# A fused transformer on one core: a second batch's shared expert moves from the second program into the first, and the addresses of the expert table with it

## The chip, the cores and the metric

The kernel runs on one core of a Trainium2 chip. The metric is the time of one launch in device microseconds. Before the change the median of 3 runs is 1389.91 us (1389.63 to 1391.88).

## What is computed

Four batches of 512 rows with 256 features go through an encoder-decoder layer (masked self-attention, cross-attention, a feed-forward net of 1024), an int8 linear layer, a second cross-attention, and a mixture of experts. All attentions have 16 heads of 16 features. The last stage is the one that the change touches. Per row `xf` (already normalised):

```
logits = xf @ router.T                 # 16 experts, the best 2 are taken, weights by softmax
gu     = xf @ gate_up[e]               # 256 -> 512, for the two experts of the row
h      = silu(gate) * up
moe    = sum over the two experts of weight * (h @ down[e])
sg, su = x @ shared_gate.T, x @ shared_up.T          # 256 -> 512 each, for every row
shared = (silu(sg) * su) @ shared_down.T             # 512 -> 256
out    = residual + moe + shared
```

All products are in f32, except attention's scores, which are stacks of bf16 parts.

## The kernel before

The kernel has two programs (two blocks of engine instructions), one behind the other.

**The first program** holds everything up to the router. Its order is written out by hand: `batch_order()` puts named operations on steps, four places to a step, and every engine walks through the same list `ORDER` and emits what is its own. A step is one key tile of one group of four heads: TensorE makes four score tiles (`score_t`, two PSUM banks in turn), ScalarE takes their exponentials, TensorE multiplies the step before with V (`values`, at place 2 of a step). Other products (projections, transposes, the router) are laid between these by `place(step, ...)` and share two PSUM banks, `bankM`: a product waits until the bank's last reader has read. `END[n]` is the last step of attention `n` (12 of them, three for each batch); attention 11 is batch 3's last. Behind it comes a tail for batch 3: transposes, the output projection, a residual add (`add` on VectorE), row statistics, normalisation (`apply` on ScalarE), a transpose (`turn`), the router's `logits`, `top`, `rank`, `route` on VectorE, and `dispatch` on GpSimd, which scatters (token, weight) pairs into the table `tag_scr` in HBM. Among these stands the shared expert of batch 0: products `gate` and `up` for each of 4 slices `m` of 128 hidden features, `swish` (SiLU on ScalarE), `hid` (VectorE multiplies), then `down` and `sadd`, which adds the product to the residual rows `acc`. `EARLY_SHARED` says how many batches are treated so.

**The second program** (`experts`) has the shared expert of the other `LATE = B - EARLY_SHARED = 3` batches on TensorE: per batch 4 slices of gate and up, with the last batch's `down_products` behind the first slice of the next. Meanwhile VectorE works out from the counts `cnt` which rows of the table belong to each of 47 tiles of 128 tokens (`places`), GpSimd reads these rows by an indirect DMA (`table`), TensorE turns them (`turn_table`, after slice `TURNED_AT`), and VectorE makes token addresses of them (`addresses`). SyncE starts the 32 transfers of all experts' weights (12.6 MB) when the table has landed, then writes `acc` to `out`. GpSimd gathers the rows of each tile (`rows(s)`, 128 rows of 1 KB), every second one of them held back by a wait on the shared expert's progress. `homes` says which buffer a tile's rows go to, `homes_free` from which slice on it is free: the buffers behind the first 33 are those of the shared expert's operands.

**The expert tiles.** When all of `hid`, the weights (`w_in`) and the first rows are there, TensorE goes through 47 tiles: gate and up product, the turn of the rows two tiles on, and the down product of the tile before. ScalarE copies the weights of the tile's expert into `w_now` two tiles ahead (`stage`), makes SiLU and scales the result by the row's weight into `yt`. GpSimd adds `yt` to `out` by an indirect DMA with accumulation, one for each tile, in order; it may start when `acc` has landed in `out` (`rows_out`). A tile of another expert than the one before may name the same rows, so SyncE lets GpSimd on (`apart`) only when the transfer of the tile before has landed; tiles of one expert follow without this wait.

## Time and profile before

| what | value |
|---|---|
| median of 3 runs | 1389.91 us |
| the profiled execution's own time | 1395.61 us |
| its span, first to last instruction | 1393.5 us |
| mean granted TensorE clock | 0.966 |
| PE busy | 1262.2 us (91%) |
| DVE busy | 872.2 us (63%) |
| ACT busy | 709.7 us (51%) |
| POOL busy | 521.4 us (37%) |
| first program ends, second begins | 1166.87 us |
| first product of an expert tile | 1242.82 us |
| first addition of an expert tile to `out` | 1253.59 us |

The busy shares are means over stages with different limits, and busy PE time contains stretches at half the clock. So the last 310 us are read by stretches below: the last steps of attention (from 1084.53), the tail of the first program (from 1120.56), the shared expert of the second program (from 1166.87) and the expert tiles (from 1242.82).

### The profile page before, as it was taken

How to read it: one execution, taken by the hardware profiler on the slowest of the kernel's cores; microseconds unless marked ns; L12 is line 12 of the kernel's file. 1: busy time of each engine (PE TensorE's matmuls, PEld its weight loads, DVE VectorE, ACT ScalarE, POOL GpSimd, SP SyncE). 2: the span in 40 equal slices, each digit the busy share in tenths (PEclk: the TensorE clock that was granted, in tenths of full speed). 3: DMA queues.
4: the chain of work that ended last, by engine and by line, in shares of the span. 5: the costliest groups of instructions: out<-in, count | busy, mean ns of one | idle time of the engine just before them, and what ended most of it. 6: DMA issues, size and time to landing. Idle time of an engine off the chain costs nothing. (4 is left out here: it accounts for less than half of the span.)

```text
span 1393.5 us, 19214 instructions
## 1 busy us (share of the span) xinstructions
PE 1262.2 (91%) x6164; PEld 616.7 (44%) x6164; DVE 872.2 (63%) x1998; ACT 709.7 (51%) x1290; POOL 521.4 (37%) x731
## 2 busy tenths in 40 slices
PE   6899989989999999999999999998899879889996
PEld 4232432323343224453443453443332344559995
DVE  5889779788877886458566567568777423112221
ACT  2345455566545654556556456455656631026663
POOL 4444251153312411326226236235323214655545
PEclk8699999999999999999999999999999989999998
DMA  8473413424331333123123123115431002963331
GB/s 254 135 241 83 148 58 81 117 69 142 111 106 24 107 92 106 35 73 106 47 62 107 46 61 107 51 57 127 132 98 33 17 15 83 367 151 40 37 36 13
DMA packets 113219, 131.58 MB, mean 94 GB/s; under 512 B 17017, under 2 KB 93305, under 8 KB 112867
## 3 DMA queue, kind: packets, MB, share of 16 engines
q1 hardware_dynamic: 102867, 119.91, 29.4%
q0 software_dynamic: 10256, 10.45, 4.8%
q8 instruction: 52, 0.85, 0.3%
q14 instruction: 44, 0.36, 0.1%
HBM read 83.25 MB, written 48.40 MB: 94 GB/s over the span
## 5 line engine op out<-in xcount | busy, mean ns | idle before, releaser
L1287 DVE TENSOR_REDUCE Mx<-bank 128x1 f32<-128x512 f32 x512 | 338.7, 684 | 206.6 <-PE bank L1021 202.8
L903 ACT ACTIVATE prob<-bank 128x512 f32<-128x512 f32 x576 | 332.2, 594 | 260.7 <-PE bank L1047 255.7
L1047 PE MATMUL bank<-QS,KS 99*128 99x512 bf16 x768 | 296.0, 387 | 39.0 <-ACT prob L903 20.6
L1021 PE MATMUL bank<-KS,QS 96*128 96x512 bf16 x768 | 298.3, 390 | 12.9 <-DVE Mx L1284 6.3
L1060 PE MATMUL bank<-prob,V 128*17 128x512 f32 x1536 | 206.6, 610 | 1.7 <-issue 1.7
L903 ACT ACTIVATE prob<-prob 128x512 f32<-128x512 f32 x192 | 120.9, 630 | 158.8 <-DVE prob L1298 157.9
L1047 PEld LDWEIGHTS bank<-QS,KS 99*128 99x128 bf16 x768 | 74.7, 98 | 233.8 <-ACT prob L903 127.1
L1021 PEld LDWEIGHTS bank<-KS,QS 96*128 96x128 bf16 x768 | 76.1, 99 | 123.7 <-issue 48.5
L1284 DVE CUSTOM_DVE_ANT_0 bank<-bank,ff_h 128x512 f32<-128x512 f32 x128 | 87.9, 696 | 21.7 <-PE bank L1021 21.1
L740 POOL TENSOR_SCALAR parts<-rest 128x512 bf16<-128x512 f32 x47 | 29.1, 620 | 184.1 <-DVE rest L1247 183.5
L1594 POOL DMA_INDIRECT out<-yt,home x47 | 73.1, 1555 | 64.7 <-SPq L1551 40.0
L726 POOL TENSOR_SCALAR shift<-mv 128x4 f32<-128x4 f32 x28 | 5.5, 196 | 239.9 <-DVE mv L1208 239.9
L1284 DVE CUSTOM_DVE_ANT_0 bank<-bank,mask 128x512 f32<-128x512 f32 x128 | 87.1, 701 | 10.7 <-PE bank L1021 10.2
L1685 PE MATMUL ebank<-xT,hid 128*128 128x128 f32 x752 | 92.2, 275 | 1.4 <-issue 0.9
L1685 PEld LDWEIGHTS ebank<-xT,hid 128*128 128x128 f32 x752 | 91.2, 192 | 4.7 <-issue 2.3
L749 POOL TENSOR_SCALAR MR<-neg 16x128 bf16<-16x128 f32 x48 | 14.3, 297 | 205.0 <-ACT neg L878 204.9
L973 PE MATMUL bank<-hT,mask 128*128 128x512 f32 x160 | 78.9, 622 | 4.6 <-DVE T L1389 3.5
L1799 DVE TENSOR_TENSOR ht<-ebank,sgt 128x256 f32<-128x256 f32 x47 | 20.0, 425 | 98.5 <-ACT sgt L1621 93.6
L1298 DVE TENSOR_TENSOR prob<-bank,ff_h 128x512 f32<-128x512 f32 x96 | 65.7, 684 | 12.6 <-PE bank L1047 12.2
L984 PE MATMUL bank<-mask,ff_h 128*128 128x256 f32 x288 | 68.1, 381 | 5.2 <-DVE rest L1247 4.4
L973 PE MATMUL bank<-hT,w_qkv 128*128 128x512 f32 x128 | 68.7, 625 | 4.1 <-DVE rest L1247 3.8
L1298 DVE TENSOR_TENSOR prob<-bank,mask 128x512 f32<-128x512 f32 x96 | 65.6, 684 | 10.0 <-PE bank L1047 9.8
(183 smaller groups left out, 1866.9 us busy)
## 6 DMA issues: line engine op xcount, KB each, us to landing
stack_scr<-parts SPq DMA_DIRECT2D x48, 384.0 KB, 2.6
QS<-stack_scr SPq DMA_DIRECT2D x47, 384.0 KB, 4.3
KS<-stack_scr SPq DMA_DIRECT2D x47, 384.0 KB, 5.2
stack_scr<-parts SPq DMA_DIRECT2D x48, 256.0 KB, 2.9
w_gu<-in_gate_up SPq DMA_DIRECT2D x16, 512.0 KB
stack_scr<-parts SPq DMA_DIRECT2D x48, 128.0 KB, 2.9
cT<-in_ctxT SPq DMA_DIRECT2D x8, 512.0 KB, 5.8
w_dn<-in_down SPq DMA_DIRECT2D x16, 256.0 KB
```

The costliest lines, as they stand in the source:

```text
L740: link(pool.tensor_scalar(s[:, 1, :], r, 1.0, 0.0, ALU.mult, ALU.add))
L903: act.activation(prob[:, u % NP_, j, :], src, ACT.Exp, scale=CAST).then_inc(exp_done, 1)
L973: ins = pe.matmul(b[:, :], w[:, kd, m * P:(m + 1) * P], src[:, kd, :], start=(kd == 0), stop=(kd == KD - 1))
L984: ins = pe.matmul(b[:, i * D:(i + 1) * D], src[:, k, t * P:(t + 1) * P], w[:, k, :], start=(k == 0), stop=(k == nk - 1))
L1021: pe.matmul(m, QS[0:STACK, h, qt * P:(qt + 1) * P], KS[0:STACK, h, :], start=True, stop=True).then_inc(s_full, 1)
L1047: pe.matmul(bankT[e % NT][:, :], KS[0:ROWS, h, kt * P:(kt + 1) * P], QS[0:ROWS, h, :], start=not on_pe, stop=True).then_inc(t_full, 1)
L1060: ins = pe.matmul(bankO[32 * j:32 * j + VW, :], V[VALUES[n]][:, kt, g * HG + j, :], prob[:, u % NP_, j, :], start=(kt == 0), stop=(kt == Q ...
L1284: dve.tensor_tensor_reduce(b, b, mb[n % 2][:, qt, :], 1.0, -3.0e38, ALU.add, ALU.max, dst).then_inc(s_read, 1)
L1287: dve.tensor_reduce(dst, b, AX.X, ALU.max).then_inc(s_read, 1)
L1298: dve.tensor_tensor(prob[:, u % NP_, j, :], bankT[e % NT][:, :], mb[n % 2][:, QT + u % QT, :], ALU.add).then_inc(t_masked, 1)
L1594: pool.indirect_dma_start(sums, bass.IndirectOffsetOnAxis(home[:, s:s + 1], 0), yt[:, s % NY, :], None, bounds_check=SLOTS - 1, oob_is_err ...
L1685: ins = pe.matmul(bank[2 + s % 2][:, m * P:(m + 1) * P], w_now[:, s % 2, k, m * P:(m + 1) * P], xT[:, s % 3, k, :], start=(k == 0), stop=( ...
```

## The change

`EARLY_SHARED` goes from 1 to 2: batch 1's shared expert leaves the second program. In the first, batch 1 takes the places in the tail that batch 0 had, and batch 0's eight products (`gate` and `up` of 4 slices) go among the last eight steps of attention 11. VectorE copies each out of its PSUM bank (`keep`: gates into `held_gate`, which lies in weights no longer used, ups into `hid[0]`). Behind attention ScalarE takes SiLU of all four gates in one instruction (`silu`), VectorE multiplies all four slices (`mul`), and batch 0's two `down` halves stand before and behind `rank`. `places()` moves behind the last `route` in the first program, with its tiles, and the fill of `table` to the first program's start; the table's read is the first instruction of GpSimd in the second program, and it is turned after the first slice and not the third. GpSimd gathers 32 tiles' rows ahead and not 47; the other 15 follow one behind each of the first 15 additions.

The diff, cut (the removed lines of `places` and of the tiles' declarations in `experts` are those that stand in the first program now):

```diff
-EARLY_SHARED = 1
+EARLY_SHARED = 2
...
             if n == NB - 1:
-                for m, step in enumerate((1.5, 2.5, 3.75, 5.5)):
-                    place(e + step, ("gate", 0, m), ("up", 0, m))
...
+                jobs = [(what, 0, m) for m in range(HT) for what in ("gate", "up")]
+                for i, job in enumerate(jobs):
+                    place(END[n] - 7 + i, job)
+                    place(END[n] - 6.75 + i, ("keep", *job))
+                place(e + 0.5, ("silu", 0))
+                place(e + 0.75, ("mul", 0))
+                for m, step in enumerate((1.5, 2.5, 3.75, 6)):
+                    place(e + step, ("gate", 1, m), ("up", 1, m))
+                for m, step in enumerate((1.75, 2.75, 4, 6.25)):
+                    place(e + step, ("swish", 1, m))
+                for m, step in enumerate((2.25, 3.25, 4.5, 6.5)):
+                    place(e + step, ("hid", 1, m))
+                for q, half, step, gap in ((0, 0, 4.75, 0.75), (0, 1, 5.5, 0.25), (1, 0, 6.75, 0.25), (1, 1, 7.25, 0.25)):
+                    place(e + step, ("down", q, half, 0), ("down", q, half, 1))
+                    place(e + step + gap, ("sadd", q, half))
...
+    if kind == "keep":
+        return "dve", [tuple(at)]
...
+        held_gate = w_qkv[:, 0:2, :, :, :].rearrange("p a w k n -> p (a w k n)")[:, 0:HT * S]
...
+                    elif kind == "silu":
+                        read_done(act, ("gate", at[0], HT - 1))
+                        act.activation(held_gate, held_gate, ACT.Silu).then_inc(gates_done, 1)
...
-                        read_done(pe, ("up", p, HT - 1))
+                        if p == 0:
+                            pe.wait_ge(hid_ready, 1)
+                        else:
+                            read_done(pe, ("up", p, HT - 1))
...
+                def places():
...
+                    dve.tensor_tensor(table_row[:, :], which[:, :], before_it[:, :], ALU.subtract).then_inc(row_ready, 1)
...
+                def keep(what, p, m):
+
+                    dst = held_gate[:, m * S:(m + 1) * S] if what == "gate" else hid[p][:, m, :]
+                    left(dve.tensor_copy(dst, bank_of((what, p, m))[:, :]), (what, p, m))
+
+                def multiply(p):
+
+                    dve.wait_ge(gates_done, 1)
+                    read_done(dve, ("up", p, HT - 1))
+                    h = hid[p].rearrange("p m n -> p (m n)")
+                    dve.tensor_tensor(h, h, held_gate, ALU.mult).then_inc(hid_ready, 1)
...
+                        if p == B - 1:
+                            places()
...
-        TURNED_AT = (0, 2)
+        TURNED_AT = (0, 0)
+        FREE, AHEAD = 10, 32
...
-        homes_free = NX * [0] + 4 * [HT] + 4 * [2 * HT] + 8 * [3 * HT]
+        homes_free = NX * [0] + 4 * [HT] + 4 * [2 * HT] + 8 * [LATE * HT]
...
-                pool.wait_ge(consts, 4)
                 pool.wait_ge(row_ready, 1)
                 pool.wait_ge(tagged, 32 * TT)
                 pool.indirect_dma_start(table[:, :, :].rearrange("s p c -> s (p c)"), None, table_of,
                                         bass.IndirectOffsetOnAxis(table_row[0:TILES, 0:1], 0),
                                         bounds_check=NE * SLOTS // P - 1, oob_is_err=False).then_inc(table_in, 16)
...
-                for s in range(TILES):
-                    if s >= ROWS_SEM and s % 2 == 0:
-                        c, i = divmod((s - ROWS_SEM) // 2, QT + HT)
+                for s in range(AHEAD):
+                    if s >= FREE and (s - FREE) % 2 == 0:
+                        c, i = divmod((s - FREE) // 2, QT + HT)
                         if i < QT:
...
+                    if AHEAD + s < TILES:
+                        rows(AHEAD + s)
...
-                places()
                 for c in range(LATE):
                     for m in range(HT):
                         n = c * HT + m
                         dve.wait_ge(sg_done, n + 1)
                         dve.tensor_tensor(hid[:, c % 2, m, :], bank[(n % 2) * 2 + 1][:, :], sg[:, n % 2, :],
                                           ALU.mult).then_inc(hid_done, 1)
-                        if n == 0:
+                        if (c, m) == TURNED_AT:
+                            addresses()
                             tile_experts()
                         if c and m == 0:
                             add_shared(c - 1)
-                        if (c, m) == TURNED_AT:
-                            addresses()
```

TensorE's queue at the tail of the first program, from the last slice before the router to the end of the program. `hT,mask` are the shared expert's gate and up products, `mask,ff_h` its down products, `w_router` the logits, `both` the ranks. Before:

```order
L973 MATMUL bank<-hT,mask 128x512 x4
L1160 MATMUL bank<-w_router,hT 128x16 x8
L1169 MATMUL bank<-both,before 128x16
...
L1169 MATMUL bank<-both,ones_b 128x16 x4
L973 MATMUL bank<-hT,mask 128x512 x4
L984 MATMUL bank<-mask,ff_h 128x256 x16
L536 UNCONDITIONAL_BRANCH
```

and now:

```order
L1000 MATMUL bank<-hT,mask 128x512 x4
L1192 MATMUL bank<-w_router,hT 128x16 x8
L1011 MATMUL bank<-mask,ff_h 128x256 x8
L1201 MATMUL bank<-both,before 128x16
...
L1201 MATMUL bank<-both,ones_b 128x16 x4
L1011 MATMUL bank<-mask,ff_h 128x256 x8
L1000 MATMUL bank<-hT,mask 128x512 x4
L1011 MATMUL bank<-mask,ff_h 128x256 x16
L558 UNCONDITIONAL_BRANCH
```

Sixteen more down products stand there, half of them between the logits and the ranks. Each f32 product of these lists is two instructions in the trace.

TensorE's queue in the last steps of attention (`QS,KS` score tiles, `prob,V` the product with V, `identf,oT` the turn of attention's output). Before:

```order
L1047 MATMUL bank<-QS,KS 128x512 x4
L1060 MATMUL bank<-prob,V 17x512 x4
L1047 MATMUL bank<-QS,KS 128x512
L1060 MATMUL bank<-prob,V 17x512 x4
L1084 MATMUL bank<-identf,oT 128x128 x4
```

and now:

```order
L1074 MATMUL bank<-QS,KS 128x512 x2
L1000 MATMUL bank<-hT,mask 128x512 x2
L1074 MATMUL bank<-QS,KS 128x512 x2
L1087 MATMUL bank<-prob,V 17x512 x4
L1074 MATMUL bank<-QS,KS 128x512
L1087 MATMUL bank<-prob,V 17x512 x4
L1111 MATMUL bank<-identf,oT 128x128 x4
```

One gate or up product of batch 0 (two rows of the list) stands among the score tiles of a step; seven more stand so in the seven steps before.

GpSimd's queue in the second program, from its start into the additions. Before:

```order
L1562 IOTA landed 1x48
L1567 DMA table<-tag_scr,table_row 47x256
L1578 DMA xr<-t_scr,token 128x256 x33
L1578 DMA hT<-t_scr,token 128x256 x8
L1578 DMA mask<-t_scr,token 128x256 x6
L1594 DMA out<-yt,home 2048x256 x47
```

and now:

```order
L1620 IOTA landed 1x48
L1630 DMA xr<-t_scr,token 128x256 x32
L1646 DMA out<-yt,home 2048x256
L1630 DMA xr<-t_scr,token 128x256
L1646 DMA out<-yt,home 2048x256
L1630 DMA hT<-t_scr,token 128x256
```

Fifteen gathers stand between additions now, and the table's read stands ahead of this piece, before the two IOTAs.

## Rows read from the trace of the kernel before

**Rows 1.** Busy time by stretch: from:to and length, engines' busy us, PEclk, DMA share, GB/s.

```profile
1084.53:1117.49 32.96, 26.30 (x149) 8.90 (x148) 12.18 (x51) 21.38 (x43) 9.00 (x14) 0.90 0.06 18
1120.56:1133.27 12.71, 10.40 (x37) 7.53 (x38) 1.37 (x3) 3.07 (x4) 0.00 (x0) 0.60 0.00 0
1150.81:1158.33 7.52, 6.67 (x23) 2.74 (x23) 2.18 (x8) 1.88 (x2) 3.98 (x4) 0.63 0.01 2
1166.87:1242.82 75.95, 67.92 (x199) 39.35 (x199) 18.70 (x47) 9.17 (x14) 43.44 (x49) 0.93 0.78 259
1253.59:1297.64 44.05, 44.05 (x342) 42.51 (x341) 11.46 (x31) 28.06 (x47) 23.39 (x16) 1.00 0.38 43
```

**Rows 2.** Timeline of POOL, expert tiles: start, us, line, operation [idle before, releaser].

```profile
1253.59 1.64 POOL L1594 DMA_INDIRECT out<-yt,home  x1 [4.24 <-DMA out<-acc]
...
1265.58 1.55 POOL L1594 DMA_INDIRECT out<-yt,home  x1 [2.85 <-SPq L1551]
...
1278.39 1.55 POOL L1594 DMA_INDIRECT out<-yt,home  x1 [1.32 <-ACT yt L1629]
1282.92 1.55 POOL L1594 DMA_INDIRECT out<-yt,home  x1 [2.98 <-SPq L1551]
1287.50 1.55 POOL L1594 DMA_INDIRECT out<-yt,home  x1 [3.02 <-SPq L1551]
1289.36 1.55 POOL L1594 DMA_INDIRECT out<-yt,home  x1 [0.30 <-ACT yt L1629]
...
1297.64 1.57 POOL L1594 DMA_INDIRECT out<-yt,home  x1 [3.01 <-ACT yt L1629]
...
1385.57 1.55 POOL L1594 DMA_INDIRECT out<-yt,home  x1 [0.30 <-issue]
```

**Rows 3.** Groups of POOL's instructions by shape, second program.

```profile
L1594 POOL DMA_INDIRECT out<-yt,home x47 | 73.1, 1555 | 64.7 <-SPq L1551 40.0 <-ACT yt L1629 14.7 <-issue 5.8
L1578 POOL DMA_INDIRECT xr<-t_scr,token x33 | 31.2, 947 | 23.3 <-issue 10.9 <-DVE token L1761 7.7 <-ACT mask L1604 4.7
```

**Rows 4.** Timeline of TensorE: a shared expert's products, and a tile's gate and up.

```profile
1177.71 7.13 PE L1661 MATMUL ebank<-hT,mask 128*128 128x512 f32 x16
1211.84 7.07 PE L1643 MATMUL ebank<-mask,hid 128*128 128x256 f32 x32
1261.17 1.03 PE L1695 MATMUL ebank<-w_dn,ht 128*128 x4
1264.04 1.03 PE L1695 MATMUL ebank<-w_dn,ht 128*128 x4
```

**Rows 5.** Timeline, table and weights in the second program.

```profile
1170.26 1.59 POOL L1567 DMA_INDIRECT table<-tag_scr,table_row  x1 [2.69 <-issue]
1175.22 0.37 SPq L1539 DMA_DIRECT2D w_gu<-in_gate_up  x1
1210.18 1.74 SPq L1540 DMA_DIRECT2D w_dn<-in_down  x1
```

**Rows 6.** Busy time by stretch, as Rows 1, around the weights' transfers.

```profile
1212.80:1224.80 12.00, 12.00 (x44) 7.93 (x43) 2.95 (x6) 0.60 (x1) 9.15 (x10) 1.00 1.07 379
1224.80:1236.80 12.00, 7.53 (x23) 4.42 (x22) 2.05 (x4) 3.20 (x4) 6.66 (x8) 0.92 0.37 110
```

**Rows 7.** Timeline, late instructions of the second program.

```profile
1200.79 0.60 ACT L1604 ACTIVATE mask<-ebank 128x512 f32<-128x512 f32 x1 [15.31 <-remote]
1232.74 0.60 ACT L1604 ACTIVATE mask<-ebank 128x512 f32<-128x512 f32 x1 [5.73 <-remote]
1247.72 0.43 DVE L1768 TENSOR_TENSOR acc<-ebank,acc 128x256 f32<-128x256 f32 x1 [5.95 <-remote]
```

**Rows 8.** Timeline, tail of the first program.

```profile
1126.93 1.28 ACT L861 ACT_TABLE_LOAD   x1
1126.97 6.46 PE L984 MATMUL bank<-w_o,hT 128*128 128x256 f32 x16 [0.69 <-ACT hT L861]
1133.56 0.69 DVE L1322 TENSOR_TENSOR acc<-bank,acc 128x512 f32<-128x512 f32 x1 [2.02 <-PE bank L984]
1150.81 0.17 PE L1169 MATMUL bank<-both,before 128*128 128x16 bf16 x1 [3.26 <-DVE both L1420]
1151.19 6.29 PE L973 MATMUL bank<-hT,mask 128*128 128x512 f32 x8
```

More of the change, by code:

```diff
@@ L251, in batch_order @@
             if n == NB - 1:
-                for m, step in enumerate((1.5, 2.5, 3.75, 5.5)):
-                    place(e + step, ("gate", 0, m), ("up", 0, m))
-                for m, step in enumerate((1.75, 2.75, 4, 6)):
-                    place(e + step, ("swish", 0, m))
-                for m, step in enumerate((2.25, 3.25, 4.5, 6)):
-                    place(e + step, ("hid", 0, m))
-                for half in range(2):
-                    place(e + 6.25 + half / 2, ("down", 0, half, 0), ("down", 0, half, 1))
-                    place(e + 6.5 + half / 2, ("sadd", 0, half))
+                jobs = [(what, 0, m) for m in range(HT) for what in ("gate", "up")]
[13 more added lines that the diff above has]
+                    place(e + step + gap, ("sadd", q, half))
     put(early, 2, ("ones", 0))
@@ L380, in build @@
     hT_last = [held(f"hT{p}", [P, KD, S], F32) for p in range(EARLY_SHARED, B)]
+    ones_e = held("ones_e", [P, NE], F32)
+    ntile = held("ntile", [P, NE], F32)
+    end = held("end", [P, NE], F32)
+    gone = held("gone", [P, NE], F32)
+    gone_tiles = held("gone_tiles", [P, NE], F32)
+    which = held("which", [P, 1], F32)
+    before_it = held("before_it", [P, 1], F32)
+    iota_p = held("iota_p", [P, 1], F32)
+    table_row = held("table_row", [P, 1], U32)
+    table = held("table", [TILES, P, 2], F32)
     tagged = lasting.enter_context(nc.semaphore("tagged"))
+    row_ready = lasting.enter_context(nc.semaphore("row_ready"))
     s_gu = mask0[:, 0:QT, :].rearrange("p (i k) n -> p i k n", i=2)
@@ L1092, in _ @@
                 for kind, *at in ORDER:
+                    if kind == "keep":
+                        continue
                     p = at[0] % B
@@ L1341, in _ @@
                 for kind, *at in ORDER:
+                    if kind == "keep":
+                        keep(*at)
+                        continue
                     p = at[0] % B
@@ L1344, in _ @@
                         tiles(*at)
+                    elif kind == "mul":
+                        multiply(*at)
                     elif kind == "stats":
@@ L1464, in experts @@
         hid = sb("hid2", [P, 2, HT, S], F32)
[L1465 removed]
+        w_now = hid[:, LATE % 2, :, :].rearrange("p (i k) n -> p i k n", i=2)
         iota_t = sb("iota_t", [1, TILES], F32)
[L1467 to L1470 removed]
         past = sb("past", [1, TILES, NE], F32)
         texp = sb("texp", [1, TILES], F32)
[L1473 to L1478 removed]
         tag = sb("tag", [P, TILES], F32)
@@ L1724, in link, with tile_experts @@
                     dve.wait_ge(chain2, links[0])
[L1726 to L1742 removed]
+                def tile_experts():
+                    dve.wait_ge(consts, 2)
                     link(dve.tensor_tensor(past[:, :, :], iota_t[0:1, :].unsqueeze(2).broadcast_to([1, TILES, NE]),
```

69 lines of the change are left out of this document (27 added, 42 removed).

## The prediction

> **What bounds the kernel now.** I first read the stretches of the last 310 us, then in each the timeline. In attention's last eight steps TensorE is busy 26.30 of 32.96 us at a mean clock of 0.90, and ScalarE 21.38: neither is full, each waits for the other in turn [rows 1]. The tail is a chain for one batch (projection, statistics, router), with the shared expert's products as filling. TensorE is idle for 3.26 us ahead of the ranks, and the level is half (1.2 GHz) for much of it: 0.60 is granted over 12.71 us and 0.63 over 7.52 us [rows 1, 8]. The second program's first 75.95 us are TensorE's: three batches of products at full pace are 3 x 21.3 = 63.9 us (32 instructions of gate and up at 7.13/16 = 0.446 us, and 32 down ones in 7.07 us [rows 4]), and 12.05 us are waits and turns. Some of these are late starts for which the trace names no local releaser [rows 7], while the DMA engines are full [rows 6].
>
> The expert tiles look like TensorE's: one every 2.87 us [rows 4]. But the end is set by GpSimd's chain of additions. A step to a tile of another expert takes 4.58 us (1282.92 to 1287.50: issue 1.55, then a wait for the landing), a step within an expert can go in 1.86 us (1287.50 to 1289.36) [rows 2]. GpSimd last waits for TensorE's pace at 1278.39; from there to 1385.57 and the end at 1393.5 nearly every step is one of these two, so what delays the sixteenth addition (1297.64) delays the end.
>
> **Attention's last steps.** Eight products of batch 0 are added, 32 instructions of 0.446 us: 14.3 us. TensorE's idle time there is 32.96 - 26.30 = 6.66 us [rows 1]. If all of it is filled the stretch grows by 14.3 - 6.7 = 7.6 us, if none, by 14.3. A mean clock of 0.90 is 6.6 us at the half level; were these at the full one, up to 3.3 us come back, so 4.3 is the low end. If a quarter of the products fall on the half level, 3.6 us are added: 17.9 at the high end. Each product stands between a step's first score tiles and the next ones, so ScalarE runs dry behind it in some steps, but it also gives TensorE work where it waited. I take 7.5, near the end at which the idle time is used. The eight copies by VectorE are as wide as the 0.69 us addition [rows 8] and find it busy 12.18 of 32.96 us [rows 1]: nothing.
>
> The Trainium skill (TensorE: Matmul & The Clock Gate, "What's actually happening") says that the throttled level is the default and activity releases it. Taken alone that would put this term at 4.3 rather than 7.5. The half levels here do stand in the stretches where TensorE waited, so the trace agrees, but a busier queue may also just move the fall.
>
> **The tail.** Batch 1's products replace batch 0's one for one. New are batch 0's down products, 7.1 us. Half of them stand in the 3.26 us gap ahead of the ranks [rows 8], which leaves 3.8. With the gap filled, the slice behind the ranks (8 instructions in 6.29 us instead of 3.6) should run at the full level: up to 2.7 us back. SiLU of four slices is at most 4 x 0.60 = 2.4 us on ScalarE behind the table load (ends 1128.2), and the multiplication at most 4 x 0.69 = 2.8 on VectorE: done by 1133.4, when the second residual addition started anyway (1133.56) [rows 7, 8]. So the first addition and TensorE hide them, but a faster projection there would buy little. `places` goes where VectorE waits for TensorE. If that cover is gone, batch 0's last bank is freed a little late: half a microsecond. Sum 3.8 - 2.7 = 1.1; I take +1, with -1 (a faster projection too) and +7 (nothing hidden) as ends.
>
> **The shared expert of the second program.** 21.3 us of products go. The table's read is GpSimd's first instruction and not 3.39 us in (1170.26 less 1166.87), so weights start 4.96 us after that, about 5.3 us into the program instead of 8.35 [rows 5]. TensorE finishes the slice ahead of the table's turn after 3.6 us and waits some 1.7 there, a new wait; behind it stand all later slices. Then two batches are 42.6 us, with the turns and last hidden slice about 46 without stalls, and 54 if each batch keeps its third of the 12.05 us. What may be late next are the weights: 32 transfers, the last issued by 1211.92, and a DMA that is full until about 1225 [rows 5, 6]. The 12.6 MB and 24 gathers of 131 KB at 367 GB/s, estimated, are 43 us; from 5.3 that is 48, and from the bound of 1225 it is 55. I take 53 us to the first tile, against 75.95: -23, with -27 and -18 as ends. Fewer gathers go ahead, 32 for 47, which helps the weights only at the end.
>
> **Gathers between additions.** Fifteen gathers of 0.95 us and 0.30 behind [rows 2, 3] now stand behind the first fifteen additions. Of the fifteen steps to the sixteenth addition, four change expert (those to 1265.58, 1282.92, 1287.50 and 1297.64): in them GpSimd waits 3.0 us for a landing [rows 2], and the gather hides. The other eleven become 1.86 + 1.25 = 3.11 us, above TensorE's 2.87. So 11 x 3.11 + 4 x 4.58 = 52.5 us instead of 44.05 [rows 1]: +8.5, and from there on nothing gives it back. The first addition came 10.8 us behind the first tile's product, because the last shared rows were added at 1247.72, some 4.4 us late [rows 7]; if that lateness goes, so do 4.4 us, which makes 4.1. Between them I take +6. If gathers lengthen the landings by their whole 1.25 us, it is 8.5 + 5 = 13.5.
>
> The Trainium skill (DMA: Bandwidth & Descriptors, "Issuing engines are not separate DMA queues") says that all issuers' transfers run on the same 16 engines and interleave. By that, an addition's landing shares them with the gather behind it: 131 KB at 367 GB/s is 0.36 us, 1.4 us in four landings. The row has the engines busy at 0.38 in this stretch [rows 1], so room is left.
>
> **Sum.** 7.5 + 1 - 23 + 6 = -8.5 us. The profiled span of 1393.5 us becomes 1385.0, its own time of 1395.61 becomes 1387.1; the median of the runs stands 5.7 us under that time, so 1389.91 - 8.5 = 1381.4 us.
>
> **Rivals.** *Attention pays it all back (slower).* In the eight steps TensorE and ScalarE pass work to each other through two banks, so a block of 1.8 us may stop ScalarE, then TensorE waits for it, and no idle time is used. For it: the waits there are for exponentials. Against it: two of the waits are of another kind, long ones for normalised rows, and a product fits whole. Its price is 17.9 there and 4 in the tail: 17.9 + 4 - 23 + 6 = +4.9, 1394.8 us. It decides once these two exceed 17 us.
>
> *The chain of additions eats it (no change).* Gathers lengthen the steps that change expert as well: 7.5 + 1 - 23 + 13.5 = -1, 1388.9 us. For it: every step is on the path to the end. Against it: 3 us of wait stand in each such step.
>
> *The gaps are worth more.* The levels rise in both stretches, the last shared rows aren't late: 4.3 + 0 - 24 + 4 = -15.7, 1374.2 us.
>
> *The change doesn't shorten the second program,* because weights bound it: at their late bound of 58 us, 7.5 + 1 - 18 + 6 = -3.5, 1386.4 us. It lies inside the forecast's own range, and the likelier the more gathers go first.
>
> **How the numbers follow.** The forecast, with the weights' case in it, has 0.56, its own range is 1376 to 1387; the larger gain has 0.15, the chain of additions 0.15, attention 0.14. About 0.2% (2.8 us) is what a measurement can tell from no change. Faster are the forecast nearly whole (0.54), the larger gain (0.15) and a fifth of the chain's case (0.03): 0.72. Within are the rest of the forecast (0.02) and most of the chain's (0.09) and a little of attention's (0.02): 0.13. Slower: 0.15. The range reaches from 1372, under the larger gain, to 1391, over the case of no change.
>
> **What would show it.** Right: the eight steps take 38 to 43 us and PEclk there is no lower; ranks follow the logits with down products between and the slice behind them takes near 3.6 us; first tile's product 50 to 56 us after the second program starts; additions of one expert 3.1 us apart up to the sixteenth, which comes some 52 us behind the first. The prediction is wrong if the steps grow by over 12 us, if the weights land after 58 us, or if the end no longer hangs on the additions.

## The result and the profile after

| | before | after |
|---|---|---|
| median of the runs side by side | 1390.89 us (1389.63 to 1392.69, 4 runs) | 1377.51 us (1376.95 to 1380.61, 4 runs) |
| the profiled execution's own time | 1395.61 us | 1376.99 us |
| its span | 1393.5 us | 1375.1 us |
| mean granted TensorE clock | 0.966 | 0.978 |

The ratio is 0.9923, with a 95% interval of 0.9895 to 0.9951: 10.7 us faster by the ratio, 13.4 by the medians. Two more comparisons of the same two programs, each with five rounds, gave 0.9908 [0.9887, 0.9928] and 0.9921 [0.9898, 0.9944], so the gain is 11 to 13 us.

These are the stretches of the changed kernel that answer to those of [rows 1]. The columns are start and end, length, then each engine's busy time and number of instructions, the granted clock, the share of the DMA engines and GB/s. The first line is attention's last eight steps, then the tail, the second program up to the first tile, from there to the first addition, and from the first to the sixteenth addition.

```profile
1080.82:1117.08 36.26, 35.06 (x182) 14.24 (x181) 16.50 (x58) 21.27 (x42) 10.60 (x16) 1.00 0.06 16
1117.08:1165.88 48.80, 39.87 (x181) 25.59 (x180) 18.64 (x64) 14.77 (x21) 9.87 (x13) 1.00 0.04 12
1165.88:1218.22 52.34, 44.55 (x134) 25.47 (x135) 12.96 (x29) 5.97 (x10) 31.35 (x34) 0.96 0.91 334
1218.22:1226.66 8.44, 8.44 (x59) 8.34 (x60) 1.51 (x4) 4.07 (x7) 1.44 (x3) 0.83 0.48 173
1226.66:1280.93 54.27, 54.27 (x418) 52.31 (x417) 13.60 (x36) 32.71 (x56) 38.75 (x30) 1.00 0.48 71
```

The profile of before that the prediction used spans 1393.5 us, and the median lies well under it. A second profile of the kernel before (experiment c2 below) spans 1386.8 us. Its stretches, cut at the same events:

```profile
1081.66:1114.76 33.10, 26.32 (x149) 9.04 (x148) 12.18 (x51) 21.39 (x43) 9.00 (x14) 0.90 0.06 18
1114.76:1164.24 49.48, 39.22 (x149) 23.66 (x148) 12.50 (x49) 12.59 (x20) 11.43 (x15) 0.83 0.04 12
1164.24:1235.72 71.48, 65.46 (x199) 37.69 (x200) 18.61 (x47) 9.06 (x14) 40.68 (x46) 0.98 0.80 272
1235.72:1248.19 12.47, 9.54 (x64) 8.44 (x63) 2.56 (x7) 4.17 (x7) 6.07 (x7) 0.91 0.75 113
1248.19:1292.76 44.57, 44.57 (x341) 43.02 (x340) 11.48 (x31) 27.58 (x47) 23.39 (x15) 0.99 0.37 43
```

Three things are to be compared. Attention's steps have the same 33 us in both profiles of before, with a clock of 0.90 in both, and 36.26 at 1.00 after. The second program's stretch to the first tile is 75.95 us in one profile of before and 71.48 in the other, so one profile alone misplaces a term by 4.5 us. And the last stretch grows by 9.7 us against the second profile, 10.2 against the first.

| stretch, us | before, first profile | before, second | after | forecast of the change | change by first / second |
|---|---|---|---|---|---|
| ahead of the eight steps | 1084.53 | 1081.66 | 1080.82 | none | -3.7 / -0.8 |
| eight steps of attention | 32.96 | 33.10 | 36.26 | +7.5 | +3.3 / +3.2 |
| tail | 49.38 | 49.48 | 48.80 | +1 | -0.6 / -0.7 |
| second program to first tile | 75.95 | 71.48 | 52.34 | -23 | -23.6 / -19.1 |
| first tile to sixteenth addition | 54.82 | 57.04 | 62.71 | +6 | +7.9 / +5.7 |
| from there to the end | 95.86 | 94.04 | 94.17 | none | -1.7 / +0.1 |
| span | 1393.5 | 1386.8 | 1375.1 | -8.5 | -18.4 / -11.7 |

The columns of the timelines below are start and duration, engine, line, operation, tiles and count, and in brackets the idle time before it and what ended it. GpSimd's additions and gathers, which answer to [rows 2]:

```profile
1226.66 1.64 POOL L1646 DMA_INDIRECT out<-yt,home  x1 [6.69 <-ACT yt L1683]
1228.60 1.01 POOL L1630 DMA_INDIRECT xr<-t_scr,token  x1 [0.30 <-issue]
1229.92 1.59 POOL L1646 DMA_INDIRECT out<-yt,home  x1 [0.30 <-issue]
...
1280.93 1.60 POOL L1646 DMA_INDIRECT out<-yt,home  x1 [2.41 <-SPq L1607]
```

A gather of 1.01 us stands behind each of the first fifteen additions, with 0.30 us of issue behind it: 1226.66 to 1229.92 is 3.26 us, and ten later steps of this kind measure 3.17 to 3.20. TensorE around the ranks and at the table's turn, which answer to [rows 8] and [rows 5]:

```profile
1144.00 3.70 PE L1011 MATMUL bank<-mask,ff_h 128*128 128x256 f32 x16
1147.53 0.17 PE L1201 MATMUL bank<-both,before 128*128 128x16 bf16 x1
...
1152.57 3.67 PE L1000 MATMUL bank<-hT,mask 128*128 128x512 f32 x8 [0.23 <-issue]
...
1172.05 0.44 PE L1704 MATMUL ebank<-identf,table 47*128 47x47 f32 x2 [2.50 <-DMA table<-tag_scr,table_row]
```

Batch 0's down products fill the 3.26 us gap ahead of the ranks, and the slice behind them takes 3.67 us, not 6.29. The last line is the new wait: TensorE stands 2.50 us for the table (forecast 1.7).

### The profile page after: what moved, and what is told of

Same layout as the page of the kernel before. It is cut to its first block and busy times, and to the rows that moved or that the text cites. A ratio compares the mean times of both kernels' runs of the same rounds, so it can differ in the third digit from the quotient of the medians.

```text
span 1375.1 us, 19222 instructions
## 1 busy us (share of the span) xinstructions
PE 1248.7 (91%) x6164; PEld 609.8 (44%) x6164; DVE 876.4 (64%) x2001; ACT 708.2 (52%) x1287; POOL 523.9 (38%) x731
## 5 line engine op out<-in xcount | busy, mean ns | idle before, releaser
L1000 PE MATMUL bank<-hT,mask 128*128 128x512 f32 x192 | 91.7, 603 | 5.7 <-DVE T L1453 3.5
L1011 PE MATMUL bank<-mask,ff_h 128*128 128x256 f32 x320 | 75.5, 381 | 6.1 <-DVE rest L1279 4.4
L1330 DVE TENSOR_TENSOR prob<-bank,mask 128x512 f32<-128x512 f32 x96 | 65.6, 684 | 10.2 <-PE bank L1074 10.0
```

The lines of the kernel that those rows point to most:

```text
L1000: ins = pe.matmul(b[:, :], w[:, kd, m * P:(m + 1) * P], src[:, kd, :], start=(kd == 0), stop=(kd == KD - 1))
L1011: ins = pe.matmul(b[:, i * D:(i + 1) * D], src[:, k, t * P:(t + 1) * P], w[:, k, :], start=(k == 0), stop=(k == nk - 1))
L1330: dve.tensor_tensor(prob[:, u % NP_, j, :], bankT[e % NT][:, :], mb[n % 2][:, QT + u % QT, :], ALU.add).then_inc(t_masked, 1)
```

## The experiments

Each was compared in five rounds with the kernel before on the same chip. "The changed kernel" has 1377.08 us in the first group, 1379.44 in the last; where a variant stands in another group than a run of the changed kernel, ratios to before are compared.

**c1 and c3: the changed kernel again.**

> The changed kernel once more, on the chip of the runs beside it. In the first comparison it was 13.4 us faster, but its profile starts the last ten steps of attention 3.7 us earlier than before's, in code that is the same. If that offset is chance (where the clock's half levels fall in the first 200 us), the gain that belongs to the change is the sum of the stretches behind it: 0 to +3 in attention, 0 in the tail, -24 up to the first tile, +6 behind it, so -14 to -15. If it is part of the change (two more small instructions at GpSimd's start), it shows again as the same offset in every profile of a kernel with these instructions.

> The changed kernel, unchanged, on the same chip as the variants above: about 1377 us, attention's last eight steps 36.3 us, first tile 52 us after the second program starts, first addition 8.5 us behind it. It is what the variants are compared with.

Measured: c1 1377.08 us (1376.16 to 1382.53, 6 runs), ratio 0.9908 [0.9887, 0.9928]; c3 1379.44 us (1377.45 to 1381.31, 6 runs), ratio 0.9921 [0.9898, 0.9944]. Eight steps 36.26 and 36.25 us, first tile 52.17 and 53.51 us into the second program, first addition 8.68 and 9.69 us behind it. The stage times of the changed kernel repeat within 1.4 us, the tail apart: 50.85 us at a granted clock of 0.93 in c1, 48.87 at 1.00 in c3. c1's forecast of -14 to -15 for the stretches behind the offset was taken against the first profile of before; against the second (c2) they sum to -10.9.

**c2: the kernel before again.**

> The kernel before, unchanged, for a second profile of it. The changed kernel and three variants of it reach attention's last ten steps at 1079.6 to 1082.7 us, the one profile of before at 1084.53; this difference arises in the first 205 us, where the change moves nothing. Theory A (chance: it comes from where the half clock levels fall): the second profile of before lies anywhere in 1079 to 1085, likely near 1081. Theory B (a part of the change sets it): 1084 to 1085 again. Also open is the rate of full DMA engines in the second program: 367 GB/s in the first profile of before, about 400 in three profiles of changed kernels. By chance it is 400 here, by the change 367. The first tile comes 76 us after the second program starts in either case.

Measured: 1388.08 us (1384.84 to 1394.24, 12 runs), ratio to itself 0.9991 [0.9971, 1.0012]. The last steps begin at 1081.66: theory A, the 3.7 us ahead of attention's last steps are no part of the change. The first tile comes after 71.48 us, not 76: a miss, since the late starts of the first profile [rows 7] are shorter here. The full DMA engines move 367 GB/s, as in the first profile, so by these profiles the higher rate after (below) comes with the change.

**e1: batch 0's eight products in the tail instead of attention.**

```diff
-                    place(END[n] - 7 + i, job)
-                    place(END[n] - 6.75 + i, ("keep", *job))
-                place(e + 0.5, ("silu", 0))
-                place(e + 0.75, ("mul", 0))
+                for m, step in enumerate((1.5, 2.5, 3.75, 5)):
+                    place(e + step, ("gate", 0, m), ("up", 0, m))
+                    place(e + step + (0.25 if m < 3 else 0), ("keep", "gate", 0, m), ("keep", "up", 0, m))
+                place(e + 5.75, ("silu", 0))
+                place(e + 6, ("mul", 0))
...
```

> Undoes one part: batch 0's eight gate and up products stand in the tail of the first program and not among attention's last steps; batch 1's come behind them. All else as in the changed kernel. Theory A (idle time of TensorE between score tiles took most of the 14.3 us, and the half levels there went): attention's steps get 3 us shorter, as before the change, the tail gets some 13 us longer, +10 against the changed kernel, which leaves -4 against before. Theory B (the gain is all of the second program and the tail would have hidden the products as well): within 3 us of the changed kernel.

Measured: 1389.69 us (12 runs), ratio 0.9985 [0.9966, 1.0003], 12.6 us over the changed kernel in the same group. Eight steps 33.30 us, tail 65.01 us:

```profile
1079.61:1112.91 33.30, 26.41 (x150) 9.11 (x149) 12.19 (x51) 21.40 (x43) 9.03 (x14) 0.90 0.06 18
1112.91:1177.92 65.01, 57.33 (x212) 34.60 (x212) 23.04 (x71) 12.15 (x19) 12.81 (x14) 0.92 0.03 9
```

Without products attention's steps are back at 0.90 and at 6.9 us of idle TensorE, and the tail pays the products at full price and more (+16.2 us for 14.3 of their own): it begins at the half level again, where the output projection takes 6.60 us for the changed kernel's 3.72. Theory A holds in kind; its +13 in the tail and +10 in all are both too small by 3. With the eight products in the tail the change brings nothing. The edit moves more than these products: batch 1's slices follow at 5.75 to 7.25 and the down halves at 7.75 to 9.25. The gap ahead of the ranks stays filled, by a slice of batch 1 (TensorE waits 0.25 us there).

**e8: half of them in attention.**

```diff
-                jobs = [(what, 0, m) for m in range(HT) for what in ("gate", "up")]
+                jobs = [(what, 0, m) for m in range(2) for what in ("gate", "up")]
-                    place(END[n] - 7 + i, job)
+                    place(END[n] - 7 + 2 * i, job)
...
+                for m, step in ((2, 1.5), (3, 2.5)):
+                    place(e + step, ("gate", 0, m), ("up", 0, m))
...
-                place(e + 0.5, ("silu", 0))
+                place(e + 2.75, ("silu", 0))
```

> The changed kernel with four of batch 0's eight gate and up products in attention (one per two steps) and four in the tail. Eight products cost the last eight steps 3.3 us (32.96 to 36.26), while TensorE's idle time there went from 6.66 to 1.20 us and the granted clock from 0.90 to 1.00. Theory A (the clock is a yield of the activity that the products add, beside the idle time): with half of them part of the idle time stays, 3 us or so, the clock is still 0.95 to 1.00, and the steps take 32 to 34 us: not longer than without products; the tail grows by 7 to 8 us against the changed kernel, total about 1382. Theory B (only filled idle time counts; the clock falls at about 0.90 unless it is all filled): the steps take 33 to 36 us at 0.90, total 1384 to 1387.

**e9: each of the eight issued twice.**

```diff
                     elif kind in ("gate", "up"):
...
+                        if p == 0:
+                            b = bank_free((kind, *at))
+                            for kd in range(KD):
+                                pe.matmul(b[:, :], s_gu[:, ("gate", "up").index(kind), kd, at[1] * P:(at[1] + 1) * P],
+                                          hT[p][:, kd, :], start=(kd == 0), stop=(kd == KD - 1))
                         columns((kind, *at), s_gu[:, ("gate", "up").index(kind), :, :], hT[p], at[1])
```

> The changed kernel with each of batch 0's eight gate and up products issued twice into the same bank, that is 32 further instructions of 0.446 us in attention's last steps. Theory A (the eight steps cost only 3.3 us because TensorE filled 5.5 us of idle time and ran at the full level; now 1.20 us of idle time is left, so the stretch is TensorE's): the steps grow by 13 to 15 us, to 49 to 51, with the clock at 1.00 and TensorE's idle time under 1.5 us, and the total by about 14. Theory B (a product fits in beside the exponentials and costs less than its own time wherever it stands): the steps grow by 3 to 8 us, to under 45, and the total by as much.

Measured, the eight steps of e8 and of e9:

```profile
1079.31:1113.71 34.40, 30.62 (x166) 11.62 (x165) 14.72 (x55) 21.41 (x43) 9.28 (x15) 0.95 0.06 17
```

```profile
1083.25:1131.52 48.27, 48.27 (x213) 20.45 (x212) 17.01 (x59) 21.36 (x43) 10.95 (x16) 1.00 0.04 12
```

With e1 and the changed kernel this is a series, in one place of the program:

| products of 1.78 us in the eight steps | steps, us | TensorE idle | granted clock |
|---|---|---|---|
| none (before twice, e1) | 33.0 to 33.3 | 6.7 to 6.9 | 0.90 |
| 4 (e8) | 34.40 | 3.8 | 0.95 |
| 8 (after) | 36.26 | 1.2 | 1.00 |
| 16 (e9) | 48.27 | 0 | 1.00 |

The first four add about 1.3 us, the next four 1.9, the next eight 12.0 of their own 14.3. The clock is 0.90 in all four profiles without products here (before twice, e1, e7) and 1.00 in all eight with eight products (the changed kernel three times, e2, e4, e5, e11, e12). Theory A of e9 holds in kind (TensorE's idle time and clock paid, and both are nearly used up at eight), though 12.0 lies under its 13 to 15. Of e8's theories the clock is A's (0.95); the length, 34.40, is above A's 32 to 34 and inside B's 33 to 36, so A was too hopeful on it. e9's total is 1389.7 us (12 runs), ratio 0.9987, 10 us over c3 in its group, for some 14 expected. e8's total is 1390.14 us (12 runs), ratio 1.0006, far above its expected 1382: its tail is 65.97 us, 17.2 over the changed one's, and not 7 to 8. In it TensorE waits 5.74 us ahead of the turn of the last rows:

```profile
1142.07 1.97 PE L996 MATMUL bank<-identf,T 128*128 128x128 f32 x8 [5.74 <-ACT T L914]
```

The four-slice SiLU and the table load that it brings were put ahead of ScalarE's last normalised rows and hold them up by 3.1 us:

```profile
1138.32 1.28 ACT L976 ACT_TABLE_LOAD   x1
1139.62 1.91 ACT L976 ACTIVATE w_qkv<-w_qkv 128x2048 f32<-128x2048 f32 x1
1141.43 0.58 ACT L914 ACTIVATE T<-acc,shift,rstd 128x256 f32<-128x256 f32 x1
```

The 8 instructions behind the wait then take 5.66 us for 3.6. So e8 says what four products cost in attention, not what four cost in a good tail.

**e7: the kernel before with the gathers' part alone.**

```diff
-                for s in range(TILES):
+                AHEAD = 32
+                for s in range(AHEAD):
...
                                             compute_op=ALU.add).then_inc(sum_out[s % NY], 16)
+                    if AHEAD + s < TILES:
+                        rows(AHEAD + s)
```

> The kernel before with one part of the change alone: 32 gathers ahead and fifteen between the additions. Theory A (each gather costs its issue in a step that waits for nothing): same-expert steps of the fifteen become 3.2 us for some 1.9 to 2.9, the sixteenth addition comes 52 to 54 us behind the first for 44, and 6 to 10 us more overall, about 1397. Theory B (the first additions come late for other reasons and TensorE's pace of 2.87 us sets them, so the gathers hide): 2 us or less more, about 1391.

Measured: 1393.27 us (12 runs), ratio 1.003 [1.0011, 1.0048]: 4.2 us slower, with 1.5 to 6.7 as ends, mostly under A's 6 to 10. The profile is of the fastest of the twelve (1387.99 us), so it shows the steps and not the loss:

```profile
1163.41:1231.83 68.42, 65.22 (x198) 37.71 (x199) 18.52 (x47) 9.06 (x14) 32.58 (x37) 0.98 0.78 269
1231.83:1238.80 6.97, 6.97 (x60) 6.87 (x59) 1.94 (x5) 3.25 (x6) 0.00 (x0) 1.00 0.24 78
1238.80:1293.11 54.31, 54.31 (x417) 52.11 (x416) 13.61 (x36) 32.85 (x56) 38.83 (x31) 1.00 0.47 71
```

The sixteenth addition comes 54.31 us behind the first (44.57 in c2): +9.7, theory A. The first addition comes 5.5 us sooner behind the first tile, 6.97 for 12.47, and the first tile itself is 3.1 us earlier. Fifteen gathers (18.8 us of GpSimd's queue, 2 MB) no longer stand ahead of that addition, but the trace of c2 doesn't show that they held it up. There GpSimd was through with them and waited for the tile's result, behind a late start of ScalarE:

```profile
1245.21 0.38 ACT L1621 ACTIVATE sgt<-ebank 128x256 f32<-128x256 f32 x1 [5.22 <-remote]
1248.19 1.64 POOL L1594 DMA_INDIRECT out<-yt,home  x1 [4.57 <-ACT yt L1629]
```

e7 has no late start behind its first tile, and 5.22 us is nearly all of the 5.5. So a gather moved between additions costs its issue there; that it gives something back ahead of the first, by fewer transfers in flight, is possible and not shown.

**e2: 37 gathers ahead in the changed kernel.**

```diff
-        FREE, AHEAD = 10, 32
+        FREE, AHEAD = 10, 37
...
-                            pool.wait_ge(y_read, c * QT + i + 1)
+                            pool.wait_ge(y_read, min(c * QT + i + 1, LATE * QT))
```

> One number: 37 gathers ahead of the additions and not 32, so ten between additions and not fifteen. In the changed kernel's trace GpSimd stands idle for 6.7 us ahead of the first addition, room for five gathers of 1.25 us. Theory A (the chain of additions sets the end, and a gather between two additions of one expert costs what it takes above the step): the first addition stays, the steps to the 12th, 13th and 14th tile go back from 3.19 to 1.86 us where the chain is behind TensorE: -4 us against the changed kernel. Theory B (the end hangs on TensorE's tiles): no change.

Measured: 1382.05 us (6 runs), ratio 0.9939 [0.9919, 0.9958]; no gain where 4 us were expected. Three steps went from 3.19 to 1.86 us and the sixteenth addition comes 51.26 us behind the first, as expected. The first addition, though, comes 13.71 us behind the first tile, for 8.4 to 9.7: a late start of ScalarE takes the 3 us back and more.

```profile
1228.42 0.38 ACT L1675 ACTIVATE sgt<-ebank 128x256 f32<-128x256 f32 x1 [8.30 <-remote]
```

**e4: `places` and the table's turn as before.** In the second program VectorE works out the rows, and the turn is behind the third slice.

```diff
-                        if p == B - 1:
-                            places()
...
-        TURNED_AT = (0, 0)
+        TURNED_AT = (0, 2)
...
+                places()
                 for c in range(LATE):
```

> Undoes one part: the table's rows are worked out at the start of the second program again, and the table is turned behind the third slice. All else as in the changed kernel. In the changed kernel TensorE waits 2.5 us for the table at the turn and 2.8 us at the first tile. Theory A (the weights' landing sets the first tile, since they start when the table has landed): weights start about 3 us later, TensorE's wait at the turn goes, the first tile comes 2 to 3 us later, +2 to +3 against the changed kernel. Theory B (TensorE's own products set the first tile): the wait at the turn goes and the first tile comes up to 2.5 us earlier.

Measured: 1380.55 us (6 runs), ratio 0.9929 [0.9909, 0.995], first tile after 54.36 us. The chain of waits, start and duration of each piece:

```profile
1207.54 12.13 DMA w_dn<-in_down
1219.66 2.07 issue
1221.73 2.49 PE ebank L1721 x16
```

The first tile waits for the landing of the last weights (1219.66) and the copy of the first tile's weights behind it. In c1 the same chain stands, shorter:

```profile
1206.67 10.23 DMA w_dn<-in_down
1216.91 2.48 issue
1219.38 2.97 PE ebank L1739 x16
```

This part of the change is worth 2 us in the profile, as theory A has it; in the medians its interval overlaps with that of the changed kernel.

**e5: weights before the table.**

```diff
-                sp.wait_ge(table_in, 16)
                 for n in range(NE):
```

> The changed kernel without SP's wait for the table ahead of the experts' weights, so that their transfers start about 5 us earlier. Theory A (the weights' landing sets the first tile, as the chain of waits of the changed kernel shows): the weights land 4 to 5 us earlier, the first tile comes by 2 to 4 us earlier (TensorE's own products are the next bound), and the total is 2 to 4 us less, near 1374. Theory B (TensorE's products and their late starts set the first tile, the weights only happen to be ready with them): the first tile stays at 52 us or comes later, since the table's read of the same engines is slowed by the weights and the turns wait for it; total 1377 to 1381.

Measured: 1379.0 us (6 runs), ratio 0.9922 [0.9895, 0.9949]: nothing gained, first tile after 52.01 us. The chain has another content:

```profile
1164.48 8.70 DMA table<-tag_scr,table_row
...
1208.53 7.17 PE ebank L1696 x32
1215.70 1.80 PE ebank L1738 x16
```

Weights are out of it. The table's read takes 8.70 us with weights beside it (4.5 to 5.2 without), TensorE waits 6.02 us for it and then goes through with hardly a break. In the changed kernel it waits 2.50 us for the table and 2.80 us ahead of the first tile, so what e5 takes away at the weights comes back at the table: theory B, by the reason that it gives. The first addition comes 63.79 us into the second program, with a late start of ScalarE (4.35 us) ahead of it.

**e11: both out of the way, and e12: the same with 37 gathers ahead.**

```diff
-        TURNED_AT = (0, 0)
+        TURNED_AT = (0, 1)
...
-                sp.wait_ge(table_in, 16)
```

> The changed kernel without SP's wait ahead of the weights, and with the table's turn behind the second hidden slice instead of the first. With the weights first alone, the table's read took 8.7 us, TensorE waited 6.0 us for it, and the first tile came at 52.0 us as before, now with no wait for weights. Theory A (the table's turn and the weights are each enough to hold the first tile at 52): with both out of the way it comes at 46 to 49 us, the chain of waits shows neither there, and the total is 3 to 5 us under the changed kernel's. Theory B (later gathers move the bound to the first tile's rows or to late starts of the other engines while the DMA engines are full): the first tile or the first addition behind it comes no earlier in sum, total within 1.5 us of the changed kernel's.

> The same with 37 gathers ahead of the additions instead of 32, so that five of the fifteen between additions go. Theory A (with weights earlier, the extra gathers no longer keep the DMA engines full behind the first tile): the first addition comes as in the run with 32, the sixteenth 3 us earlier, and the total is 3 us under that run's. Theory B (extra gathers ahead delay the first addition, whatever the weights do, as in the run with 37 and weights behind the table): the first addition comes 3 to 5 us later and the total is the same within 1.5 us.

Measured: e11 1377.24 us (1374.88 to 1379.58, 6 runs), ratio 0.9908 [0.9885, 0.9931]; e12 1380.65 us (6 runs), ratio 0.993 [0.9902, 0.9958]; the changed kernel in the same group 1379.44, 0.9921. First tile after 45.28 and 45.48 us, 6 to 9 us sooner than in the changed kernel and the other variants: theory A for the two bounds. But the first addition comes 13.59 and 17.68 us behind it, so it comes 58.87 us into the second program for the 60.8 to 63.2 of the changed kernel, and e12's 63.16. In both it is TensorE that loses the time. In e11 it stops three times inside the first tile's 16 products, for 2.37, 1.13 and 0.44 us, with no releaser on record, and then the second tile's 16 fall on the half level, 3.63 us for 1.95:

```profile
1213.20 1.17 PE L1738 MATMUL ebank<-xT,hid 128*128 128x128 f32 x9
1216.74 0.27 PE L1738 MATMUL ebank<-xT,hid 128*128 128x128 f32 x1 [2.37 <-issue]
1218.14 0.27 PE L1738 MATMUL ebank<-xT,hid 128*128 128x128 f32 x1 [1.13 <-issue]
1218.85 0.82 PE L1738 MATMUL ebank<-xT,hid 128*128 128x128 f32 x5 [0.44 <-issue]
```

```profile
1219.67:1223.38 3.71, 3.71 (x20) 3.66 (x19) 1.06 (x3) 1.44 (x2) 2.80 (x4) 0.54 0.66 199
```

e12 has stops of 1.71, 1.13 and 1.13 us at the same place. VectorE has a late start too, of 8.02 us in e11 and 8.03 us in e12 at the same instruction (the line is of e11):

```profile
1218.89 1.09 DVE L1805 TENSOR_TENSOR acc<-ebank,acc 128x256 f32<-128x256 f32 x3 [8.02 <-remote]
```

GpSimd's next gathers need that addition's home to be free, and they stand ahead of the first addition to `out` in its queue. Yet in e11 GpSimd is through with them and waits 2.51 us for `yt`. In e12 `yt` is there at 1230.13 and the last of nine gathers ends at 1231.24, so there the queue adds 1.1 us at most. The addition of e11:

```profile
1226.79 1.64 POOL L1645 DMA_INDIRECT out<-yt,home  x1 [2.51 <-ACT yt L1682]
```

Theory B for the end, then: 7 us at the first tile became 2 to 4 at the first addition. Whether e11 beats the changed kernel is not settled: 2.2 us by the medians, with intervals that overlap. e12 has no gain over e11, theory B of its own by the outcome; its first addition is 4.3 us later, most of it because `yt` is (61.7 for 57.9 us into the second program), not because of five more gathers in the queue.

## Why the prediction came out as it did

The direction was right, and the time of 1377.51 us lies inside the range of 1372 to 1391 and of the forecast's own, 1376 to 1387. It is 3.9 us under the forecast of 1381.4. Attention and the tail came out better and the second program worse, so that the sum is this near is in part luck.

**Attention's last steps: the term that was mis-sized.** Forecast +7.5 (from 4.3 to 17.9), measured +3.2 to 3.3. Its first half was right: the idle time is nearly all used, 6.66 to 1.20 us, so 5.5 for the 6.7 allowed. The error was the choice of "none comes back" for the half level. Before, the half level is one stretch behind a wait of 2.15 us for exponentials:

```profile
1091.71 0.61 PE L1047 MATMUL bank<-QS,KS 99*128 99x512 bf16 x1 [2.15 <-ACT prob L903]
```

```profile
1091.47:1098.09 6.62, 5.72 (x20) 2.07 (x21) 0.68 (x2) 4.68 (x10) 0.00 (x0) 0.51 0.00 0
```

TensorE is busy for 5.72 us of it; at the full level half of that, 2.9 us, comes back (an estimate from this row, for the 3.3 at most of the prediction). The changed kernel waits 1.05 us at that place and stays at the full level. The series of e1, e8 and the changed kernel, 0.90, 0.95, 1.00, shows that this goes with the amount of product work added and isn't chance. The prediction weighed this rule of the Trainium skill (TensorE: Matmul & The Clock Gate, "What's actually happening"), put the term at 4.3 by it, and did not take it; the trace agrees with the rule.

So of the products' own 14.3 us, 5.5 are filled idle time, about 2.9 the clock, 3.3 are the growth measured, and 2.6 remain. These fit instructions that started out of a wait before and don't now: a score tile alone is busy for 0.39 us, in a row they start 0.22 us apart. This last part is argued from durations alone. The lines are of the changed kernel's steps, then of before's first profile:

```profile
L1074 PE MATMUL bank<-QS,KS 99*128 99x512 bf16 x32 | 10.7, 382 | 1.0 <-ACT prob L928 1.0
```

```profile
L1047 PE MATMUL bank<-QS,KS 99*128 99x512 bf16 x32 | 12.0, 407 | 5.7 <-ACT prob L903 5.0 <-issue 0.5
```

The columns are line, names, shapes and count, busy time and mean ns of one, and idle time before with its releasers. TensorE's waits for exponentials went from 5.0 to 1.0 us. The rival in which the products stop ScalarE fell: it is busy 21.27 us of these steps, as before.

**The tail.** Forecast +1 (from -1 to 7), measured -0.6, with +1.4 in c1. Down products stand in the gap ahead of the ranks and the slice behind them is back at 3.67 us, as said. But the number came out near by two parts that were not forecast so: from the ranks to the end it is 2.3 us more than before, for the 1.1 reckoned, and the ranks come 2.9 us sooner, since the tail's first products run at the full level too (granted clock 1.00 for 0.83 over the tail). The projection, 6.46 us before [rows 8], is

```profile
1124.70 3.72 PE L1011 MATMUL bank<-w_o,hT 128*128 128x256 f32 x16 [0.74 <-ACT hT L886]
```

The prediction had this as its low end only and held that it would buy little. e1 shows what it costs where the eight products stand in the tail: +16.2.

**The second program.** Forecast: first tile after 53 us, ends 49 and 58; measured 52.34, 52.17 and 53.51. As a time this was right. As a difference, -23, it was too large by 4 against the second profile of before: the 75.95 us that it was taken from hold 12.05 us beside the products' 63.9, the second profile's 71.48 only 7.6. The forecast named the late starts [rows 7], took them in full on the before side, and left 10.4 us beside the products' 42.6 on the after side, where 9.7 were measured. The first profile's own time stands 5.7 us over the median of its runs, the second's (1388.9) lies at that of its group (1389.4), so the median doesn't hold the late starts of the first in full. e11's 45.28 us agree with the 46 without stalls.

The table's wait is 2.50 for 1.7 us. In c1's chain the weights land at 1216.91, 1.7 us after TensorE is through with its products (1215.23): the first tile waits for them, which the prediction had as a rival inside its range. e4, e5 and e11 show that both bounds were there.

**Gathers between additions.** Forecast: same-expert steps of 3.11 us, 52.5 us from the first to the sixteenth addition; measured 3.19 and 54.3, since the four that change expert are 0.2 us longer on average and the others 0.08 to 0.09. Of the 4.4 us that the prediction held against it, 2.3 and 4.0 came: the first addition is 8.4 us behind the first tile for 10.8 and 12.5. The reason was only in part the one given, a late VectorE. In the first profile of before ScalarE is late at the same time, by 12.22 us, and in the second, where VectorE isn't late there, ScalarE is by 5.22; the changed kernel has neither, but runs its first 3.41 us of tiles at a clock of 0.57. Together +5.7 to +7.9 for +6. e7 shows this part alone costs 4 us on the kernel before. The rule on shared transfer engines (the Trainium skill, DMA: Bandwidth & Descriptors, "Issuing engines are not separate DMA queues") would have added 1.4 us in four landings; 54.27 us measured for 52.5 has 0.9 from the issue (eleven steps of 3.19 and not 3.11) and 0.8 in the four steps with landings, so the trace leaves room for about half of it.

**The sum,** against the second profile of before: 3.2 - 0.7 - 19.1 + 5.7 = -10.9, with -0.8 ahead and +0.1 behind it is the -11.7 of the spans; by the medians -13.4, -12.8 (c1) and -11.5 (c3). Forecast -8.5: attention 4.3 better, tail 1.7 better, second program 3.9 worse.

## What to carry to other kernels

Work moved into a stage where TensorE waits costs less than its own time twice over, by the idle time it fills and by the clock that it keeps up; count both, up to the point where no idle time is left, and nearly full price behind that (12.0 us for 14.3 in e9). Where a term is the difference of two stretches, take the before side from two profiles, or price both sides with the same late starts. And when one bound goes, follow the gain down to what ends the kernel: here some 7 us at the first tile were 2 to 4 at the first addition, because TensorE stopped inside the first tile and ran the next at the half level.

## What was not expected of the hardware

**Late starts.** While the DMA engines are full, an engine often starts an instruction 4 to 8 us late with no local releaser, as in [rows 7]. Some repeat: in the changed kernel it is ScalarE's last gate slice each time. The line is of after; in c1 it is 5.23 us:

```profile
1206.87 0.60 ACT L1658 ACTIVATE mask<-ebank 128x512 f32<-128x512 f32 x1 [4.34 <-remote]
```

It is 5.16 us in c3, 5.17 in e2, 5.22 in e1, 4.32 in e8 and 5.20 in e9, and e11 and e12 have 8.02 and 8.03 at another instruction. So a change of order moves them, and part of what a variant wins or loses is this. Others don't repeat: in the first profile of before ScalarE is late by 15.31 us once [rows 7], which the second has nowhere, and at the first tile by 12.22 us for 5.22. The page of the profile names two DMA queues "instruction"; in this late start and in c1's they have no packet, so these traces don't speak for a fetch of instructions held up by the weights. The cause stays open.

**The rate of full DMA engines.** In 20 us while they are full they move 367, 367 and 368 GB/s in both profiles of before and in e7, and 397 to 402 in the changed kernel, c1, c3, e4, e5, e8 and e11 and in e1, all with two batches in the first program. From the second program's start to the first addition e7 and the changed kernel move the same 19 MB (251 GB/s over 75.39 us, 312 over 60.78). What of the change does this was not found.

**One read of the table,** 4.46 to 5.17 us in the changed kernel, where no weights are in flight yet, is 8.70 us when they are (e5) and 7.73 in e11.
